# A cross-attention and expert kernel: the last sum of a group in two halves, reciprocals multiplied in one operation, and the work on x one slot later

## The chip, the core and the metric

The kernel runs on one core of a Trainium2 chip. The metric is device time of one execution, in microseconds. PE is the matrix engine, DVE, ACT and POOL are the vector, scalar and GpSimd engines, and SP issues most of the DMAs. A "block" is 128 rows.

## What is computed

Cut to what matters (four batches, 512 tokens of width 512, a context of 1601 rows):

```python
def attention(q, k, v):
    scores = jnp.einsum('bqhd,bkhd->bhqk', q, k) * scale
    probs = jax.nn.softmax(scores, axis=-1)
    return jnp.einsum('bhqk,bkhd->bqhd', probs, v)
q = rms_norm(linear(x, q_w, q_b), norm_q_w)            # 16 heads of 32
k, v = rms_norm(linear(ctx_txt, k_w, k_b), norm_k_w), linear(ctx_txt, v_w, v_b)
k_img, v_img = rms_norm(linear(ctx_img, ...)), linear(ctx_img, ...)
out = linear(attention(q, k_img, v_img) + attention(q, k, v), o_w, o_b)
x = x + out(_layernorm(x), ctx_2048)
x = x + moe(_layernorm(x))                             # 32 experts, top 4, and a shared expert
```

## The kernel before

The attention part works through the four batches (`one_pass`, p = 0; a second pass runs only for data with extreme scores). Each batch has a projection (`project` on each engine) and an attention stage (`attention` on PE, `exponentials` on ACT, `sums_and_results` on DVE). The expert part follows. Every engine has its own instruction stream, written out by hand, and semaphores join them; an engine never passes over an instruction that waits. The order of the work is therefore the order in which the calls stand in each engine's loop.

**Projection.** It has 17 slots, i = 0 to 16. Thirteen hold a block of the context (`KV_SLOT` = 0 to 7, 9, 11, 13, 15, 16), from which a key block and, one slot later, a value block are made; four (`Q_SLOT` = 8, 10, 12, 14) hold a block j = 0 to 3 of x, from which the queries are made. All operands of the products are split into a high and a low f16 part, so a product of 128 rows is 12 matmuls.

- The product of slot i is `key(i)` on PE. For a slot of x it waits for `x_out`, the landing of the turned block (`rows_turned` in `key`), and reads it from `xt`.
- Its result is taken out of PSUM by DVE in `key_raw(i)` (L796), squared and summed by ACT in `key_square(i)` (L628), scaled by POOL in `key_scale(i)` (L533, L536), normalized by DVE in `key_norm(i)` (L809, one slot later), cast by ACT in `key_high(i)` (L623), and its low part is made by DVE in `key_low(i)` (L815), which in DVE's stream stands in slot i+1 behind `key_raw(i+1)`. SP then turns it with a DMA transpose, `turn_key(i)` (L382), in slot i+1 too.
- The context block's own low part is `ctx_low` (L777) on DVE.
- A block of x goes through `x_stats` (L821, L822) on DVE, `x_scale` (L540, L541) on POOL, `x_normed` (L826) on DVE, `x_high` (L634) on ACT, `x_low` (L830) on DVE and `turn_x` (L387) on SP. In SP's slot the transpose of x stands behind `turn_key(i-1)`.
- In batches 1 to 3 the results of the batch before are finished in the same slots. `weigh` (L835, L836, L839) in slots 3 to 6 multiplies the numerators of a group, of image and text keys, by the reciprocals that a DMA has spread, and adds both; `out_low` (L844) follows. The output product, the residual's load (L364), the layer norm and the stores (L368, L372, L398) and a transpose (L393) stand in slots 8 to 16.

**Attention stage.** For each of four groups of four heads it passes over 13 key blocks (n = 0 to 12), so 52 steps s. PE makes the scores two steps ahead (`scores`, L1215), ACT the exponentials in two halves into one of four buffers (L718), PE the numerators (`weighted`, L1221). DVE adds the exponentials of the text keys up (`acc`, L972 and L975), so that PE can sum them over the rows with few matmuls (`text_part`, L1261). Image keys have their own sum (`image_sum`, L936) and their own copy of the numerators (L954). At n = 12 DVE waits for PE's last numerators, copies them out of PSUM (L963), which lets PE start the next group in that bank (`a_nt`), and adds the last exponentials (L975), which frees their buffer for ACT (`a_sum`). In batch 3 DVE also converts weights of the shared expert (`ffn_weight`, L869, L870) between groups.

Of the kernel before, what the change touches and what calls it, by code (L numbers as in the profile page):

```python
# [30 lines left out]
NG = HEADS // 4  # L31
# [132 lines left out]
def attention_program(nc, m, d, x1_dram, x2_dram, r_dram, table, out, s_turned, s_xr):  # L164

    with ExitStack() as ctx:
# [168 lines left out]
        def _(sp):  # L335
# [49 lines left out]
            def turn_x(bb, j):  # L385
                sp.wait_ge(x_lo, xn(bb, j))
                sp.dma_start_transpose(xt[:, j, :].rearrange("p (a k) -> p a k", k=P),  # L387
                                       xs[j % 2].rearrange("p s n -> p (s n)")).then_inc(x_out[j % 2], 16)
# [29 lines left out]
            def one_pass(p):  # L418
# [16 lines left out]
                for bb, b in passes(p):  # L435
                    if b > 0:
                        sp.wait_ge(c_lo, kvn(bb, 0))
                        load_ctx(bb, b, 2)
                    upto(sp, a_den, bb * NG)
                    q = out_batch(bb - 1) if b else None  # L440
                    for i in range(SLOTS):
                        if b > 0 and i == 1:
                            store_sums(bb - 1)
                        k = KV_AT.get(i)
                        if k is not None and k + 2 < KT and k > 0 and (b > 0 or k != 2):
                            sp.wait_ge(c_lo, kvn(bb, k))
                            load_ctx(bb, b, k + 2)
                        if b == 0 and k == 1:
                            sp.wait_ge(c_lo, kvn(bb, 2))
                            load_ctx(bb, b, 4)  # L450
                        if i == 4:
                            load_x(bb, b, 1)
                        if b == 0 and i == 1:
                            load_x(bb, b, 0)
                            load_weight(WQ)
                            if p == 0:
                                load_vec(QB, "qb", s_vq)
                                load_vec(QW, "qw", s_vq)
                        if bb == 0 and i == 4:
                            load_weight(WO)  # L460
                            sp.wait_ge(s_vq, 32)
                            load_vec(OB, "ob", s_vq)
                            sp.dma_start(vb2[:, 0, :], d["vb"]).then_inc(s_vq, 16)
                            sp.dma_start(vb2[:, 1, :], d["vib"]).then_inc(s_vq, 16)
                            sp.dma_start(mark[:, :, :], d["mark"]).then_inc(s_vq, 16)
                        if bb == 0 and i == 6:
                            sp.wait_ge(s_z0, 3)
                            zero = mxrow[:, :, :].rearrange("p g q -> p (g q)").bitcast(F32)
                            sp.dma_start(table[T:T + DUMMY, :], zero[:, 0:TROW]).then_inc(s_zero, 16)
                            sp.dma_start(out[T:T + DUMMY, :], zero[:, 0:D]).then_inc(s_zero, 16)  # L470
                        if i == 1 and b > 0:
                            load_x(bb, b, 0)
                        if i in (5, 6) and b > 0:
                            residual(q, b - 1, i - 5)
                        if i >= 1:
                            turn_key(bb, i - 1)
                        if b > 0 and i - 1 in LOW_SLOT:
                            store_turned(q, b - 1, LOW_SLOT.index(i - 1))
                        if b > 0 and i in NORM_SLOT:
                            j = NORM_SLOT.index(i)  # L480
                            store_norm(q, b - 1, j)
                            if j + 2 < QT:
                                residual(q, b - 1, j + 2)
                        if b > 0 and i in LOW_SLOT:
                            turn_out(q, LOW_SLOT.index(i))
                        if i in (5, 7, 9, 11):
                            turn_x(bb, (i - 5) // 2)
                        if b > 0 and i - 1 in O_SLOT:
                            store(q, b - 1, O_SLOT.index(i - 1))
                    if b + 1 < B:  # L490
                        first_loads(bb + 1, b + 1)
                    turn_key(bb, SLOTS - 1)
                    if b > 0:
                        store_turned(q, b - 1, QT - 1)
# [20 lines left out]
        def _(pool):  # L515
# [39 lines left out]
            def one_pass(p):  # L555
                for bb, b in passes(p):
                    for i in range(SLOTS):
                        if i in (3, 5, 7, 9):
                            x_scale(bb, (i - 3) // 2)
                        key_scale(bb, i)  # L560
                        if b > 0 and i in O_SLOT:
                            add_bias(out_batch(bb - 1), O_SLOT.index(i))
                        if b > 0 and i - 1 in O_SLOT:
                            out_scale(out_batch(bb - 1), O_SLOT.index(i - 1))
# [19 lines left out]
        def _(act):  # L584
# [67 lines left out]
            def project(p, bb, b):  # L652
# [8 lines left out]
                for i in range(SLOTS):  # L661
# [11 lines left out]
                    if b > 0 and WEIGH + 1 <= i < WEIGH + 1 + NG:  # L673
                        out_high(q, i - WEIGH - 1)
                        if i - WEIGH - 1 < 2:
                            spread(bb, i - WEIGH + 1)
                    if i in (4, 6, 8, 10):
                        x_high(bb, (i - 4) // 2)
                    if b == 0 and i <= 1:
                        ctx_high(bb, 2 + i)  # L680
                    key_square(bb, i)
# [63 lines left out]
        def _(dve):  # L745
# [86 lines left out]
            def weigh(q, g):  # L832

                dve.wait_ge(s_rb[g % 2], 64 * (2 * q + g // 2 + 1))
                image = own(dve.tensor_tensor(nums[:, g, 1, :], nums[:, g, 1, :], rb[:, g % 2, 1, :], ALU.mult))  # L835
                dve.tensor_tensor(nums[:, g, 0, :], nums[:, g, 0, :], rb[:, g % 2, 0, :], ALU.mult).then_inc(a_mt, 1)  # L836
                dve.wait_ge(d_link, image)
                dve.wait_ge(a_mt, gn(q, g))
                dve.scalar_tensor_tensor(nums[:, g, 0, :], nums[:, g, 1, :], vbias[:, g:g + 1], nums[:, g, 0, :],  # L839
                                         ALU.add, ALU.add).then_inc(a_at, 1)  # L840
# [32 lines left out]
            def project(p, bb, b):  # L873
                q = out_batch(bb - 1) if b else None
                for i in range(SLOTS):
# [7 lines left out]
                        out_norm(q, NORM_SLOT.index(i))  # L883
                    if b > 0 and i in LOW_SLOT[:QT - 1]:
                        norm_low(q, LOW_SLOT.index(i))
                    if i in (3, 5, 7, 9):
                        x_stats(bb, (i - 3) // 2)
                    if i in (4, 6, 8, 10):
                        x_normed(bb, (i - 4) // 2)
                    if i in (5, 7, 9, 11):  # L890
                        x_low(bb, (i - 5) // 2)
                    if bb == 0:
                        if i == 0:
                            dve.wait_ge(s_vi, 32)
# [46 lines left out]
            def sums_and_results(p, bb, b):  # L941
                fl = lambda t: t.rearrange("p h q -> p (h q)")
                for g in range(NG):
# [13 lines left out]
                    for n in range(4, KT):  # L957
                        s = s0 + n
                        dve.wait_ge(a_exp, unit(bb, 2 * s + 1))
                        cur = fl(prob[:, s % PROBS, :, :])  # L960
                        if n == KT - 1:
                            dve.wait_ge(a_av, step(bb, s))
                            dve.tensor_copy(nums[:, g, 0, :], ps[:, NUM, :]).then_inc(a_nt, 1)  # L963
                        if b == B - 1 and g == NG - 1 and n >= KT - PRODUCT_SUMS:
                            continue
                        if n == 4:
# [1147 lines left out]
```

## Time and profile before

| | us |
|---|---|
| Median of 3 runs | 1189.96 (1187.46 to 1190.88) |
| The profiled execution, its own time | 1194.59 |
| Its span, first to last instruction | 1192.8 |
| PE busy | 1116.2 (94%) |
| DVE busy | 856.9 (72%) |
| ACT busy | 650.6 (55%) |
| POOL busy | 202.1 (17%) |
| Mean granted clock of PE | 0.995 |

Busy times are shares of one execution whose stages have different limits, so they are to be read by stage. The projections end at about 92, 295, 498 and 701 us, the attention stages at about 201, 404, 607 and 814; the expert part takes the rest. PE's matmuls are pipelined, and a busy PE isn't PE at its peak. A wait names the instruction that came last by the profile.

### The profile page before, as it was taken

To read this page: it belongs to the slowest core of one execution; us is meant where nothing else is said; L and a number is where in the kernel's file an instruction comes from. 1 tells how busy PE (TensorE), PEld (TensorE's weight loads), DVE (VectorE), ACT (ScalarE), POOL (GpSimd) and SP (SyncE) were. 2 spreads that over 40 slices of the span, in tenths; PEclk is the share of its full clock that TensorE was granted. 3 is DMA by queue.
4 is the path that set the end of the run, shared out by engine and by line. 5 is a ranking of instruction groups with operands and counts; after the bars stand their busy time and mean duration, and the time that the engine had idled before them with its cause. 6 is when DMAs were issued, how large, how long until landed. Compare 5 with 4: busy or idle time off the path is not lost. (4 is left out here: it accounts for less than half of the span.)

```text
span 1192.8 us, 21823 instructions
## 1 busy us (share of the span) xinstructions
PE 1116.2 (94%) x8948; PEld 415.7 (35%) x8948; DVE 856.9 (72%) x1056; ACT 650.6 (55%) x916; POOL 202.1 (17%) x307
## 2 busy tenths in 40 slices
PE   7899999999999989999999999887999989999996
PEld 3342223344222334322233432222544433333332
DVE  6777889897898988788889879997789842222221
ACT  5559997444999644699955469883311121221121
POOL 1220000243000024300002430002100021333442
PEclk9999999999999999999999999999999999999999
DMA  8851000768200096900028780104813337999742
GB/s 299 199 109 43 2 2 10 194 135 201 54 2 2 20 228 136 203 8 2 2 72 194 171 215 31 36 3 136 359 60 109 113 113 285 348 317 313 215 62 33
DMA packets 142860, 150.15 MB, mean 126 GB/s; under 512 B 108833, under 2 KB 109089, under 8 KB 137761
## 3 DMA queue, kind: packets, MB, share of 16 engines
q1 hardware_dynamic: 135328, 131.57, 38.1%
q0 software_dynamic: 5120, 10.82, 4.9%
q10 hardware_dynamic: 2304, 6.29, 2.2%
q8 instruction: 72, 1.18, 0.4%
q14 instruction: 36, 0.29, 0.1%
HBM read 101.96 MB, written 21.51 MB: 104 GB/s over the span
## 5 line engine op out<-in xcount | busy, mean ns | idle before, releaser
L718 ACT ACTIVATE work<-ps 128x1024 f32<-128x1024 f32 x384 | 372.3, 1022 | 30.7 <-PE ps L1215 15.0
L1221 PE MATMUL ps<-work,vals 128*32 128x512 f32 (+2 forms) x1664 | 220.3, 600 | 3.8 <-DVE nums L963 2.1
L1072 PE MATMUL ps<-wts,work 128*128 128x512 f16 x864 | 194.9, 379 | 11.1 <-DVE work L777 10.7
L1215 PE MATMUL ps<-quer,keys 32*128 32x512 f16 x2496 | 171.9, 377 | 22.2 <-ACT work L718 14.9
L975 DVE TENSOR_TENSOR work<-work 128x2048 f32<-128x2048 f32 x64 | 146.6, 2291 | 6.2 <-ACT work L718 0.5
L975 DVE TENSOR_TENSOR attn<-attn,work 128x2048 f32<-128x2048 f32 x62 | 142.0, 2290 | 5.4 <-ACT work L718 0.5
L1072 PEld LDWEIGHTS ps<-wts,work 128*128 128x128 f16 x864 | 83.3, 98 | 118.7 <-issue 19.3
L2040 PE MATMUL ps<-wring,xgt 128*80 128x512 f32 x256 | 114.9, 592 | 0.0
L1866 DVE COPY xgt<-ps 128x320 f32<-128x320 f32 x32 | 15.7, 491 | 137.8 <-PE ps L2031 137.8
L1072 PE MATMUL ps<-wts,hl 128*128 128x512 f16 x432 | 101.1, 386 | 12.0 <-DVE wts L759 7.3
L533 POOL TENSOR_SCALAR small<-small 128x1 f32<-128x1 f32 x68 | 20.5, 301 | 534.9 <-ACT work L628 534.9
L1215 PEld LDWEIGHTS ps<-quer,keys 32*128 32x128 f16 x2496 | 46.3, 92 | 183.4 <-ACT work L718 149.9
L623 ACT CAST work<-work 128x512 f16<-128x512 f32 x68 | 42.0, 617 | 114.5 <-DVE work L809 114.4
L809 DVE SCALAR_TENSOR_TENSOR work<-work,small,vec 128x512 f32<-128x512 f32 (+1 forms) x72 | 59.4, 824 | 20.2 <-POOL small L536 20.2
L628 ACT ACTIVATE work<-work 128x512 f32<-128x512 f32 x68 | 42.8, 630 | 47.6 <-DVE work L796 47.6
L2055 PE MATMUL ps<-wring,ht 128*80 128x512 f32 x128 | 62.2, 608 | 6.4 <-ACT ht L1608 3.6
L1534 POOL DMA_INDIRECT out<-yf,idx x32 | 45.4, 1420 | 131.7 <-DMA out<-yf,idx 102.3
L1072 PEld LDWEIGHTS ps<-wts,hl 128*128 128x128 f16 x432 | 41.8, 99 | 68.2 <-issue 20.9
L2040 PEld LDWEIGHTS ps<-wring,xgt 128*80 128x80 f32 x256 | 38.4, 150 | 71.1 <-issue 70.9
L1613 ACT ACTIVATE yf<-ps,xg 80x512 f32<-80x512 f32 x32 | 21.9, 683 | 71.0 <-PE ps L2055 47.7
L1221 PEld LDWEIGHTS ps<-work,vals 128*32 128x32 f32 (+2 forms) x1664 | 38.7, 108 | 58.8 <-issue 52.7
L1608 ACT COPY ht<-ps 128x160 f32<-128x160 f32 x32 | 9.3, 291 | 77.8 <-PE ps L2048 77.8
(221 smaller groups left out, 1402.5 us busy)
## 6 DMA issues: line engine op xcount, KB each, us to landing
wring<-in_wx SPq DMA_DIRECT2D x32, 1536.0 KB, 9.1
raw<-in_ctx SPq DMA_DIRECT2D x52, 256.0 KB, 3.3
rb<-sums_inverse ACTq DMA_DIRECT2D x48, 128.0 KB, 3.8
work<-in_x SPq DMA_DIRECT2D x8, 512.0 KB, 4.8
table<-nums SPq DMA_DIRECT2D x16, 256.0 KB, 2.5
work<-in_x SPq DMA_DIRECT2D x12, 256.0 KB, 3.5
x<-work SPq DMA_DIRECT2D x12, 256.0 KB, 2.6
x2t_rows<-nums SPq DMA_DIRECT2D x12, 256.0 KB, 2.5
```

Source lines behind the costliest of these rows:

```text
L623: act.copy(stack[i % 2][:, 0, :], kraw[i % 2]).then_inc(k_hi, 1)
L628: act.activation(junk, kraw[i % 2], ACT.Square, accum_out=ssq[i % 2]).then_inc(k_sq, 1)
L718: act.activation(prob[0:rows, s % PROBS, 2 * half:2 * half + 2, :], ps[0:rows, 2 * pair:2 * pair + 2, :], ACT.Exp, scale=SCALE, bias=pad i ...
L809: ins = dve.scalar_tensor_tensor(kraw[i % 2][a:z, :], kraw[i % 2][a:z, :], rin[i % 2][a:z, :], vec[a:z, weight, :], ALU.mult, ALU.mult)
L975: dve.tensor_tensor(acc, acc, cur, ALU.add).then_inc(a_sum, 1)
L1072: mm = pe.matmul(out, lhs(a, c)[:, cols], wts[:, w, z, c * D:(c + 1) * D], start=(k == 0), stop=(k == len(steps) - 1))
L1215: mm = pe.matmul(ps[:, 2 * pair + h % 2, :], k[h * HD:(h + 1) * HD, :], q[h * HD:(h + 1) * HD, :], start=(e == 0), stop=(e == len(terms) - 1))
L1221: return pe.matmul(ps[h * HD:(h + 1) * HD, NUM, :], vals[a:z, ORDER[n], g * P + h * HD:g * P + (h + 1) * HD], prob[a:z, s % PROBS, h, :], ...
L1534: pool.indirect_dma_start(out=out[:, :], out_offset=bass.IndirectOffsetOnAxis(ap=idx[:, n:n + 1], axis=0), in_=yf[n % RESULTS][:, :], in_o ...
L1613: act.activation(yf[n % RESULTS][:, :], ps[0:CAP, 2 + n % 2, :], ACT.Copy, scale=xg[n % GATHERS][:, D + n:D + n + 1]).then_inc(m_yf, 1)
L2040: mm = pe.matmul(ps[0:CAP, 7 if n % 2 == 0 else 0, :], xgt[n % 2][:, c, :], wring[n % RING][:, c * D:(c + 1) * D], start=(c == 0), stop=(c ...
L2055: mm = pe.matmul(ps[0:CAP, 2 + n % 2, :], ht[n % 2][:, c, :], wring[n % RING][:, (NC + c) * D:(NC + c + 1) * D], start=(c == 0), stop=(c = ...
```

## The change

1. At n = 12 the addition of 2048 columns becomes two of 1024, one ahead of the wait for PE's numerators and their copy, one behind. Only the second signals `a_sum`. The last group of batch 3, which has no such addition, stays as it was.
2. In `weigh` one multiplication of 128x1024 takes the place of two of 128x512.
3. The steps of a block of x move one slot on, on DVE, POOL, ACT and SP. PE's slots of x stay.

```diff
--- before.py
+++ after.py
@@ -483,8 +483,8 @@
                                 residual(q, b - 1, j + 2)
                         if b > 0 and i in LOW_SLOT:
                             turn_out(q, LOW_SLOT.index(i))
-                        if i in (5, 7, 9, 11):
-                            turn_x(bb, (i - 5) // 2)
+                        if i in (6, 8, 10, 12):
+                            turn_x(bb, (i - 6) // 2)
                         if b > 0 and i - 1 in O_SLOT:
                             store(q, b - 1, O_SLOT.index(i - 1))
                     if b + 1 < B:
@@ -555,8 +555,8 @@
             def one_pass(p):
                 for bb, b in passes(p):
                     for i in range(SLOTS):
-                        if i in (3, 5, 7, 9):
-                            x_scale(bb, (i - 3) // 2)
+                        if i in (4, 6, 8, 10):
+                            x_scale(bb, (i - 4) // 2)
                         key_scale(bb, i)
                         if b > 0 and i in O_SLOT:
                             add_bias(out_batch(bb - 1), O_SLOT.index(i))
@@ -674,8 +674,8 @@
                         out_high(q, i - WEIGH - 1)
                         if i - WEIGH - 1 < 2:
                             spread(bb, i - WEIGH + 1)
-                    if i in (4, 6, 8, 10):
-                        x_high(bb, (i - 4) // 2)
+                    if i in (5, 7, 9, 11):
+                        x_high(bb, (i - 5) // 2)
                     if b == 0 and i <= 1:
                         ctx_high(bb, 2 + i)
                     key_square(bb, i)
@@ -832,9 +832,8 @@
             def weigh(q, g):
 
                 dve.wait_ge(s_rb[g % 2], 64 * (2 * q + g // 2 + 1))
-                image = own(dve.tensor_tensor(nums[:, g, 1, :], nums[:, g, 1, :], rb[:, g % 2, 1, :], ALU.mult))
-                dve.tensor_tensor(nums[:, g, 0, :], nums[:, g, 0, :], rb[:, g % 2, 0, :], ALU.mult).then_inc(a_mt, 1)
-                dve.wait_ge(d_link, image)
+                both = nums[:, g, :, :].rearrange("p t q -> p (t q)")
+                dve.tensor_tensor(both, both, rb[:, g % 2, :, :].rearrange("p t q -> p (t q)"), ALU.mult).then_inc(a_mt, 1)
                 dve.wait_ge(a_mt, gn(q, g))
                 dve.scalar_tensor_tensor(nums[:, g, 0, :], nums[:, g, 1, :], vbias[:, g:g + 1], nums[:, g, 0, :],
                                          ALU.add, ALU.add).then_inc(a_at, 1)
@@ -883,12 +882,12 @@
                         out_norm(q, NORM_SLOT.index(i))
                     if b > 0 and i in LOW_SLOT[:QT - 1]:
                         norm_low(q, LOW_SLOT.index(i))
-                    if i in (3, 5, 7, 9):
-                        x_stats(bb, (i - 3) // 2)
                     if i in (4, 6, 8, 10):
-                        x_normed(bb, (i - 4) // 2)
+                        x_stats(bb, (i - 4) // 2)
                     if i in (5, 7, 9, 11):
-                        x_low(bb, (i - 5) // 2)
+                        x_normed(bb, (i - 5) // 2)
+                    if i in (6, 8, 10, 12):
+                        x_low(bb, (i - 6) // 2)
                     if bb == 0:
                         if i == 0:
                             dve.wait_ge(s_vi, 32)
@@ -959,8 +958,15 @@
                         dve.wait_ge(a_exp, unit(bb, 2 * s + 1))
                         cur = fl(prob[:, s % PROBS, :, :])
                         if n == KT - 1:
+                            parted = not (b == B - 1 and g == NG - 1)
+                            if parted:
+                                dve.wait_ge(a_sum, added(bb, g, n - 5))
+                                dve.tensor_tensor(acc[:, 0:2 * L], acc[:, 0:2 * L], cur[:, 0:2 * L], ALU.add)
                             dve.wait_ge(a_av, step(bb, s))
                             dve.tensor_copy(nums[:, g, 0, :], ps[:, NUM, :]).then_inc(a_nt, 1)
+                            if parted:
+                                dve.tensor_tensor(acc[:, 2 * L:], acc[:, 2 * L:], cur[:, 2 * L:], ALU.add).then_inc(a_sum, 1)
+                                continue
                         if b == B - 1 and g == NG - 1 and n >= KT - PRODUCT_SUMS:
                             continue
                         if n == 4:
```

On SP, slots 9 and 10 of the projection of batch 1. L387 turns a block of x, L382 a key or query block, L372 stores to the table, L364 loads the residual. Before:

```order
L382 DMA_TRANSPOSE quer<-work 128x8x128 [waits k_lo]
L387 DMA_TRANSPOSE work<-work 128x8x128 [waits x_lo]
L368 DMA x<-work 128x512 [waits o_out]
L382 DMA_TRANSPOSE keys<-work 128x8x128 [waits k_lo]
L372 DMA table<-nums 128x512 [waits n_norm]
L364 DMA work<-in_x 128x512 [waits s_st0,n_norm]
L368 DMA x<-work 128x512 [waits o_out]
```

And now:

```order
L382 DMA_TRANSPOSE quer<-work 128x8x128 [waits k_lo]
L368 DMA x<-work 128x512 [waits o_out]
L382 DMA_TRANSPOSE keys<-work 128x8x128 [waits k_lo]
L372 DMA table<-nums 128x512 [waits n_norm]
L364 DMA work<-in_x 128x512 [waits s_st0,n_norm]
L387 DMA_TRANSPOSE work<-work 128x8x128 [waits x_lo]
L368 DMA x<-work 128x512 [waits o_out]
```

The transpose of x's block 2 went from behind the query block of slot 8 to behind the key block of slot 9 and two further DMAs.

On DVE, slots 9 and 10 of the same projection (L848, L853, L854, L859 of the change are L849, L854, L855, L860 of before). Before:

```order
L821 BN_STATS small<-work 128x6
L822 BN_AGGR small<-small 128x2
L830 TENSOR_TENSOR work<-work 128x512
L796 SCALAR_TENSOR_TENSOR work<-ps,vec 128x512
L815 TENSOR_TENSOR work<-work 128x512
L849 SCALAR_TENSOR_TENSOR work<-ps,work 128x512
L854 BN_STATS small<-work 128x6
L855 BN_AGGR small<-small 128x2
L777 TENSOR_TENSOR hl_62<-raw,hl_62 128x512
L809 SCALAR_TENSOR_TENSOR work<-work,small,vec 128x512
L860 TENSOR_SCALAR nums<-work,small 128x512
L826 TENSOR_SCALAR work<-work,small 128x512
```

And now:

```order
L796 SCALAR_TENSOR_TENSOR work<-ps,vec 128x512
L815 TENSOR_TENSOR work<-work 128x512
L848 SCALAR_TENSOR_TENSOR work<-ps,work 128x512
L853 BN_STATS small<-work 128x6
L854 BN_AGGR small<-small 128x2
L777 TENSOR_TENSOR hl_62<-raw,hl_62 128x512
L809 SCALAR_TENSOR_TENSOR work<-work,small,vec 128x512
L859 TENSOR_SCALAR nums<-work,small 128x512
L821 BN_STATS small<-work 128x6
L822 BN_AGGR small<-small 128x2
L830 TENSOR_TENSOR work<-work 128x512
L796 SCALAR_TENSOR_TENSOR work<-ps,vec 128x512
```

The next row of the first piece is the L796 of slot 10. The statistics and the subtraction for x stood ahead of the L796 of slot 9 and now stand ahead of that of slot 10, where the normalizing (L826) was.

On DVE, the first group end of batch 0. Before:

```order
L972 TENSOR_TENSOR work<-work 128x2048
L975 TENSOR_TENSOR work<-work 128x2048 x7
L963 COPY nums<-ps 128x512
L975 TENSOR_TENSOR work<-work 128x2048
L936 TENSOR_TENSOR image<-work 128x2048
```

And now:

```order
L978 TENSOR_TENSOR work<-work 128x2048
L981 TENSOR_TENSOR work<-work 128x2048 x7
L964 TENSOR_TENSOR work<-work 128x1024
L966 COPY nums<-ps 128x512
L968 TENSOR_TENSOR work<-work 128x1024
L935 TENSOR_TENSOR image<-work 128x2048
```

The copy of the numerators now has a half addition on each side.

## Rows read from the trace of the kernel before

**Rows 1.** Windows: a projection, an attention stage; columns as in the first row.
```profile
core 0: us, PE busy (x) PEld busy (x) DVE busy (x) ACT busy (x) POOL busy (x), PEclk, DMA share, GB/s
200.70:295.50 94.80, 90.16 (x461) 39.30 (x458) 80.55 (x121) 40.65 (x88) 29.94 (x54) 1.00 0.69 163
310.00:400.00 90.00, 86.12 (x1192) 23.98 (x1192) 81.10 (x42) 84.81 (x88) 0.00 (x0) 1.00 0.02 5
```

**Rows 2.** PE's timeline, projection of batch 1: start, us, instructions, [idle before <-releaser].
```profile
241.89 2.75 PE L1072 MATMUL ps<-wts,work 128*128 128x512 f16 x12 [1.18 <-DVE work L777]
...
247.06 5.34 PE L1072 MATMUL ps<-wts,work 128*128 128x512 f16 x24
...
260.01 5.34 PE L1072 MATMUL ps<-wts,work 128*128 128x512 f16 x24
...
267.78 2.75 PE L1072 MATMUL ps<-wts,work 128*128 128x512 f16 x12
```

**Rows 3.** SP's timeline (its DMA issues), the same projection.
```profile
244.09 2.29 SPq L382 DMA_TRANSPOSE keys<-work  x1
...
265.85 1.26 SPq L382 DMA_TRANSPOSE keys<-work  x1
...
267.83 0.38 SPq L364 DMA_DIRECT2D work<-in_x  x1
```

**Rows 4.** The transposes of x (L387): last line of that line's own view.
```profile
DMA to landing us min/median/max: 3.1/3.2/5.1
```

**Rows 5.** DVE's timeline, the same projection, slots 6, 9 and 10.
```profile
243.38 0.68 DVE L815 TENSOR_TENSOR work<-work 128x512 f16<-128x512 f32 x1
...
257.00 0.68 DVE L821 BATCH_NORM_STATS2 small<-work 128x6 f32<-128x512 f32 x1
...
258.39 0.68 DVE L796 SCALAR_TENSOR_TENSOR work<-ps,vec 128x512 f32<-128x512 f32 x1
...
264.08 0.54 DVE L826 TENSOR_SCALAR work<-work,small 128x512 f32<-128x512 f32 x1
264.54 0.69 DVE L796 SCALAR_TENSOR_TENSOR work<-ps,vec 128x512 f32<-128x512 f32 x1
265.14 0.68 DVE L815 TENSOR_TENSOR work<-work 128x512 f16<-128x512 f32 x1
```

**Rows 6.** PE's timeline, projection of batch 0.
```profile
59.56 7.93 PE L1072 MATMUL ps<-wts,work 128*128 128x512 f16 x36 [0.70 <-DVE work L777]
...
70.86 2.75 PE L1072 MATMUL ps<-wts,work 128*128 128x512 f16 x12 [0.39 <-DMA work<-work]
```

**Rows 7.** SP's timeline, projection of batch 0.
```profile
50.53 1.71 SPq L382 DMA_TRANSPOSE keys<-work  x1
```

**Rows 8.** DVE's timeline, projection of batch 0.
```profile
61.04 0.68 DVE L815 TENSOR_TENSOR work<-work 128x512 f16<-128x512 f32 x1
```

**Rows 9.** DVE's timeline, first group end of batch 0.
```profile
122.97 0.69 DVE L963 COPY nums<-ps 128x512 f32<-128x512 f32 x1 [0.76 <-PE ps L1221]
123.58 2.28 DVE L975 TENSOR_TENSOR work<-work 128x2048 f32<-128x2048 f32 x1
```

**Rows 10.** ACT's timeline behind the same group end.
```profile
125.98 1.94 ACT L718 ACTIVATE work<-ps 128x1024 f32<-128x1024 f32 x2 [0.32 <-DVE work L975]
...
132.91 1.94 ACT L718 ACTIVATE work<-ps 128x1024 f32<-128x1024 f32 x2 [0.83 <-PE ps L1215]
```

**Rows 11.** PE's timeline, end of group 1 in batch 3.
```profile
761.48 1.07 PE L1221 MATMUL ps<-work,vals 128*32 128x512 f32 x8 [1.03 <-DVE nums L963]
```

**Rows 12.** PE's timeline behind its two longest waits after the start.
```profile
829.07 2.04 PE L1900 MATMUL ps<-rcp,sel 128*128 128x512 f32 x2 [5.48 <-PEq L166]
...
984.59 0.47 PE L2031 MATMUL ps<-identf,xg 80*128 80x80 f32 x4 [2.70 <-DVE xgt L1866]
```

**Rows 13.** Windows over the same two places; the next to last columns hold clock.
```profile
828.00:832.00 4.00, 2.93 (x4) 1.41 (x5) 2.04 (x4) 0.62 (x1) 1.28 (x8) 0.61 0.18 29
984.00:988.00 4.00, 3.42 (x14) 1.56 (x15) 0.93 (x3) 0.00 (x0) 0.00 (x0) 0.74 0.74 215
```

## The prediction

> **What bounds the kernel now.** I read the stretches first, because the two kinds of stage have different limits. Between two attention stages lies a projection of 94.8 us in which PE is busy for 90.16 us; in attention ACT is busy for 84.81 of 90.00 us, PE for 86.12 and DVE for 81.10 [rows 1]. So a projection is a PE stage: a change counts there if it makes PE wait longer or shorter. Attention is an ACT stage with PE and DVE close behind.
>
> Next, PE's timeline in the projection of batch 1 [rows 2]. Slots are numbered i = 0 to 16. The row at 241.89 is key(7), and its 1.18 us of waiting ends with a DVE subtraction (L777): in slots 3 to 6 DVE is the slower engine. The row at 247.06 is key(8), the first product that reads a turned block of x; 260.01 is key(10) and 267.78 is key(12), which read blocks 1 and 2. None of these waits. Call their starts T8, T10 and T12.
>
> Then SP's queue [rows 3] with the landing times [rows 4]: a turned block of x lands 3.2 us after its issue. The row at 265.85 is the turning of key(9) in slot 10, which waits for key_low(9) on DVE, the row at 265.14 [rows 5]. It is followed by two more DMAs of slot 10, the last at 267.83 for 0.38 us.
>
> **The move of x by a slot.** Per block it moves five steps: two DVE statistics and the POOL scale behind them, the DVE normalizing, ACT's cast, DVE's subtraction, and the transpose on SP. Nothing is added or removed, but PE's use of the blocks stays in slots 8, 10, 12 and 14. The transpose must now follow the turning of a key in its own, later slot: turn_x(2) used to follow turn_key(8), which waits for key_low(8), and now follows turn_key(9). And key_low(9) stands on DVE behind key_raw(10), which needs PE's key(10) to be finished. So the new loop is: key(10) on PE, key_raw(10) and key_low(9) on DVE, turn_key(9) and turn_x(2) on SP, landing, key(12).
>
> Its smallest length in batch 0, where nothing else is queued: 2.75 (product) + 0.05 + 0.60 + 0.68 (raw, low) + 0.03 + 1.28 (one transpose's issue and the step to the next) + 3.2 (landing) + 0.15 (PE's start after its releaser) = 8.74 us. PE itself needs three products of 2.59 from one x product to the next, 7.77 us. The loop therefore exceeds PE's work. In batches 1 to 3 two further DMAs lie in it, about 1.0 us, so at least 9.7 us.
>
> Batches 1 to 3, with the clock of batch 1:
> - T8. From slot 3 to key_low(5) in slot 6 DVE has one normalizing less, 0.46, and three merged multiplications, 0.06 each (below). key_low(5) moves from 243.38 to about 242.8 [rows 5]. turn_key(5) is issued at 243.5 and takes 1.24 at best (here 2.29 [rows 3]); turn_x(0) follows at 244.8, lands at 248.0, and PE starts at 248.15 instead of 247.06: +1.1, or +2.1 with the long transpose. DVE's relief up to key(7), one pair of statistics and subtraction less (1.39, see T12) and 0.1 of the multiplications, so 1.5 us at most, is swallowed whole, since PE now waits behind it for block 0.
> - T10 is natural, 261.1: block 1 lands at about 258.5.
> - T12. In slots 8 to 10, ahead of key_raw(10), DVE carried one pair of statistics and subtraction, 1.39 (257.00 to 258.39), and two normalizings of 0.46 (264.08 to 264.54) [rows 5]; now two pairs and one normalizing, 0.93 more. Key_raw(9) waits 0.33 for the later key(9). So key_low(9) ends at 267.1 instead of 265.82, turn_key(9) follows, turn_x(2) is issued 2.4 later at 269.5 behind the table's store and the residual's load, lands at 272.7, and PE starts at 272.9 instead of 267.78: +5.1. As some of DVE's short waits will close up, I take **4.8 per batch, 14.4 for three**. The bounds are +1.9 (no backlog on DVE, T10 unmoved: 9.7 against 7.77) and +6.1.
> - T14 needs block 3 at about 285.5 and has it by 285.4: nothing more, though without reserve.
>
> Batch 0 [rows 6 to 8]. Here block 2 already ends a wait of 0.39 before T12 (70.86). Block 0 now follows turn_key(5), issued at 50.53 and then, with a pair in place of a normalizing ahead of it, at about 51.1: it lands at 55.6, T8 is 55.75 (today about 53.5). Block 1 now follows key_low(7), 61.04 plus 1 of extra x work plus 0.68, so 62.8; plus 1.3 to its issue and 3.2 to its landing: T10 is 67.4 instead of 62.15 (59.56 and one product). Two loops of 8.74 follow: T14 is 84.9 instead of 78.6 (three products after 70.86). **+6.3**; bounds +3.3 (T8 at 55.75 and three smallest loops, 82.0) and +7.
>
> **The addition in two halves.** At a group's end DVE waits 0.76 for PE, copies the numerators, then adds 2.29 us [rows 9]. A half addition (128x1024) should take 1.22: 0.68 for 512 columns [rows 5] and 2.28 for 2048 give 0.53 per 512 more. It fills the 0.76 and overshoots: the copy moves from 122.97 to 123.44, +0.47, the addition's end from 125.86 to 125.27, -0.59. ACT's wait of 0.32 for the addition [rows 10] seems to go. But PE starts the next group's numerators 0.15 after the copy, so the scores of the next tile but one end at about 126.1 instead of 125.6, and ACT gets them at 126.16 instead of 125.98. The next two tiles are then within 0.05 of today, and the 0.83 that ACT waits for scores at 132.91 follows PE, which is 0.03 later. Ten group ends: **0**, bounds -0.3 and +0.2 each. At the end of a batch the last sum is not what PE waits for: 0. In batch 3, where the FFN weights' conversion leaves DVE behind, PE already waits 1.03 for the copy [rows 11]; there the copy comes 1.23 later, and the next group, which runs at DVE's pace, loses 0.95. Two such places: **+1.9**, bounds 0 and 2.5.
>
> **Reciprocals in one operation.** 12 multiplications fewer; from the first one to the sum behind them took 1.39 and will take 1.22 + 0.11: 0.06 each. It lies in slots 3 to 6, already counted, and is swallowed with the relief: 0.
>
> **The clock.** A stall of four microseconds may have a price of its own. After 5.48 us without matmuls the granted clock of 828 to 832 is 0.61, most of it at the lower of the two levels (1.2 GHz instead of 2.4); after a wait of 2.70 it is 0.74 in the stretch that holds the end of the wait [rows 12, 13]. The first is (1 - 0.61) x 4 = 1.6 us of PE's work lost. The new stalls are about 3.9 us long, one in each batch (268.9, when PE has done its work, to 272.8; 63.5 to 67.4 in batch 0).  A stall of 3.9 after dense work lies between, so I take two of four: **+3.2**, bounds 0 and 6.4.
> The Trainium skill ("TensorE: Matmul & The Clock Gate", Part 1) says that the throttled state is the default and that activity releases it. By that rule every one of the four stalls loses the clock, and the sum would be 3.2 higher; both rows of this trace agree with it.
>
> **Sum.** 6.3 + 14.4 + 1.9 + 3.2 = 25.8, less about 0.8 for the last wait of a projection, where DVE will have caught up a little: +25. Against the profiled execution's own time of 1194.59 that is 1219.6; the median of the runs, 1189.96, lies 4.6 lower, and the same step gives **1215**.
>
> **Rivals.**
> 1. Mild: DVE has no backlog left when key(10) ends, because the stall itself gives it time. The loops then have their smallest lengths, 3.3 + 3 x 1.9 = 9: 1199. For it: DVE idles 15% of the projection [rows 1]. Against: the order on DVE puts the moved pair directly ahead of key_raw(10), so time gained earlier doesn't help. Chance 0.12.
> 2. Faster: DVE's relief reaches PE, 1.5 us in three projections, and twelve waits of 0.32 for the addition go: -8.3, 1181.7. It decides at one point: turn_x(2) must be issued before 264.4 to land before 267.78 (and turn_x(0) before 243.7). Against it, key(10) itself ends at 262.76 and 2.6 us of DVE and SP work lie between. Chance 0.04, with all that could be faster.
> 3. The gains and the late blocks cancel within 0.3%, about what a measurement of this kernel can tell from no change. It needs the late blocks to cost 3 us or so in all, less than batch 0's smallest loops alone. Chance 0.04.
> 4. The clock is lost at each stall, and the long transposes come too: 1221. This is the upper part of my own case.
>
> The forecast has 0.80. The range, 1203 to 1224, takes in all of it and half of the mild rival. Faster 0.04, same 0.04, slower 0.92.
>
> **What would show it.** PE's wait ahead of key(12) is released by the DMA that writes a block of x, 3 to 5 us in each batch, and in batch 0 ahead of key(10) too. The wait ahead of key(7) is below 0.3. In attention the copy follows a half addition without a wait, ACT's 0.32 is about the same or moved, and the two last group ends of batch 3 are longer. I am wrong if no wait of PE on such a DMA passes 1 us, or if projections are shorter than 94 us.

## The result, and the profile after

The change takes **1228.92 us** (median of 6 runs, 1226.3 to 1232.46) and the kernel before 1191.18 in the same session (6 runs, 1187.46 to 1192.05): a ratio of **1.0323 [1.0299, 1.0348]**. The direction is the forecast's; the time lies 13.9 us above the 1215 and 4.9 above the upper end of the range, 1224. The profiled execution has an own time of 1230.48 and a span of 1228.7.

The page of the changed kernel, busy time of the engines, the granted clock in 40 slices, and the group of the projection's products:

```profile
PE 1130.3 (92%) x8948; PEld 418.7 (34%) x8948; DVE 858.7 (70%) x1059; ACT 652.2 (53%) x916; POOL 205.2 (17%) x307
...
PEclk9999999988999999899999999999899999999999
...
L1078 PE MATMUL ps<-wts,work 128*128 128x512 f16 x864 | 207.8, 397 | 32.8 <-DMA work<-work 25.3
```

The wait that had a total of 0.4 us (once, in batch 0 [rows 6]) is now the largest of the projection: eight times, 25.3 us together, for the DMA that turns a block of x. A ninth, ahead of key(8) in batch 0, is named `issue` in the rows; but SP issued turn_x(0) at 52.97, 3.31 us before that wait ends, so it is of the same kind:

```profile
56.28 9.62 PE L1078 MATMUL ps<-wts,work 128*128 128x512 f16 x36 [2.04 <-issue]
67.94 5.34 PE L1078 MATMUL ps<-wts,work 128*128 128x512 f16 x24 [2.04 <-DMA work<-work]
```

The matmuls of the group also have more busy time, 397 ns each where it was 379. Windows of the changed kernel, the projection of batch 1 and the stretches behind its two stalls (columns as in [rows 1]):

```profile
208.03:314.19 106.16, 95.44 (x461) 40.31 (x458) 80.70 (x118) 40.97 (x86) 31.05 (x54) 0.94 0.64 146
254.00:258.00 4.00, 2.19 (x6) 0.82 (x7) 3.40 (x7) 3.19 (x7) 0.74 (x2) 0.62 0.89 175
258.00:262.00 4.00, 4.00 (x12) 1.36 (x11) 2.31 (x6) 0.76 (x2) 1.08 (x2) 0.53 0.01 2
282.00:286.00 4.00, 1.12 (x3) 0.44 (x4) 2.78 (x6) 2.36 (x6) 0.74 (x2) 0.53 1.13 261
286.00:290.00 4.00, 4.00 (x13) 1.49 (x12) 1.43 (x3) 0.61 (x1) 0.00 (x0) 0.62 1.11 206
```

The projection took 94.80 us before [rows 1] and takes 106.16: 6.1 us more in which PE does nothing, and 5.3 more in which the same 461 matmuls take longer, since the clock is granted at 0.94. PE's timeline of the changed kernel, the same projection:

```profile
250.16 2.75 PE L1078 MATMUL ps<-wts,hl 128*128 128x512 f16 x12
255.81 8.27 PE L1078 MATMUL ps<-wts,work 128*128 128x512 f16 x24 [2.90 <-DMA work<-work]
...
271.69 5.34 PE L1078 MATMUL ps<-wts,work 128*128 128x512 f16 x24
276.87 2.75 PE L1078 MATMUL ps<-wts,hl 128*128 128x512 f16 x12
284.88 4.81 PE L1078 MATMUL ps<-wts,work 128*128 128x512 f16 x12 [5.26 <-DMA work<-work]
```

The row at 255.81 is key(8), 271.69 is key(10) and 284.88 key(12). There are **two** stalls in the batch, not one, and matmuls behind each run at the lower level: 24 take 8.27 us (5.34 in [rows 2]), 12 take 4.81 (2.75). What SP and DVE do ahead of them in the changed kernel, SP first:

```profile
250.71 1.24 SPq L382 DMA_TRANSPOSE keys<-work  x1
252.39 1.24 SPq L387 DMA_TRANSPOSE work<-work  x1
...
277.71 1.24 SPq L382 DMA_TRANSPOSE keys<-work  x1
278.99 0.57 SPq L372 DMA_DIRECT2D table<-nums  x1
279.66 0.38 SPq L364 DMA_DIRECT2D work<-in_x  x1
280.09 1.24 SPq L387 DMA_TRANSPOSE work<-work  x1
```

```profile
250.00 0.68 DVE L815 TENSOR_TENSOR work<-work 128x512 f16<-128x512 f32 x1
...
274.54 0.55 DVE L859 TENSOR_SCALAR nums<-work,small 128x512 f32<-128x512 f32 x1 [0.44 <-POOL small L547]
275.00 0.69 DVE L821 BATCH_NORM_STATS2 small<-work 128x6 f32<-128x512 f32 x1
...
276.39 0.69 DVE L796 SCALAR_TENSOR_TENSOR work<-ps,vec 128x512 f32<-128x512 f32 x1
277.00 0.68 DVE L815 TENSOR_TENSOR work<-work 128x512 f16<-128x512 f32 x1
```

The loop of the forecast is there step by step. Key(10) ends at 274.3; the moved pair (275.00) keeps key_raw(10) until 276.39; key_low(9) ends at 277.68; turn_key(9), the table's store and the load of the residual put turn_x(2) at 280.09, 2.38 behind turn_key(9) (2.4 was said); PE starts 4.79 later. That last step was said to be 3.35.

### The profile page after: what moved, and what is told of

Its sections match the earlier page's. It is cut to its first block and busy times, and to the rows that moved or that the text cites. A ratio compares the mean times of both kernels' runs of the same rounds, so it can differ in the third digit from the quotient of the medians.

```text
span 1228.7 us, 21814 instructions
## 1 busy us (share of the span) xinstructions
PE 1130.3 (92%) x8948; PEld 418.7 (34%) x8948; DVE 858.7 (70%) x1059; ACT 652.2 (53%) x916; POOL 205.2 (17%) x307
## 3 DMA queue, kind: packets, MB, share of 16 engines
q8 instruction: 72, 1.18, 0.4%
## 5 line engine op out<-in xcount | busy, mean ns | idle before, releaser
L1078 PE MATMUL ps<-wts,work 128*128 128x512 f16 x864 | 207.8, 397 | 32.8 <-DMA work<-work 25.3
L981 DVE TENSOR_TENSOR work<-work 128x2048 f32<-128x2048 f32 x56 | 128.4, 2292 | 6.3 <-DVE work L981 0.5
L981 DVE TENSOR_TENSOR attn<-attn,work 128x2048 f32<-128x2048 f32 x55 | 126.0, 2292 | 5.4 <-ACT work L718 0.4
L533 POOL TENSOR_SCALAR small<-small 128x1 f32<-128x1 f32 x68 | 23.0, 338 | 575.5 <-ACT work L628 575.5
L796 DVE SCALAR_TENSOR_TENSOR work<-ps,vec 128x512 f32<-128x512 f32 (+1 forms) x72 | 49.4, 686 | 34.4 <-PE ps L1078 34.1
L2046 PEld LDWEIGHTS ps<-wring,xgt 128*80 128x80 f32 x256 | 38.4, 150 | 71.1 <-issue 70.9
```

The source lines that it names most:

```text
L796: ins = dve.scalar_tensor_tensor(kraw[i % 2][a:z, :], bank[a:z, :], 1.0 / WS, vec[a:z, bias, :], ALU.mult, ALU.add)
L981: dve.tensor_tensor(acc, acc, cur, ALU.add).then_inc(a_sum, 1)
L1078: mm = pe.matmul(out, lhs(a, c)[:, cols], wts[:, w, z, c * D:(c + 1) * D], start=(k == 0), stop=(k == len(steps) - 1))
L2046: mm = pe.matmul(ps[0:CAP, 7 if n % 2 == 0 else 0, :], xgt[n % 2][:, c, :], wring[n % RING][:, c * D:(c + 1) * D], start=(c == 0), stop=(c ...
```

## The experiments

All ratios are to the kernel before, run on the same chip. The table has the stages of the profiled executions, in us. A projection is taken from the last exponential of one batch to the first of the next. "Lower" is the time at the 1.2 GHz level up to the end of the projection of batch 3, attention left out.

| kernel | start to attention 0 | projections 1, 2, 3 | attention 3 | lower |
|---|---|---|---|---|
| before | 92.6 | 94.80, 94.32, 94.14 | 113.22 | 0 |
| the change | 99.6 | 106.16, 103.11, 102.74 | 115.55 | 34.1 |
| x's move alone | 99.2 | 103.85, 103.41, 102.77 | 113.20 | 23.9 |
| halves alone | 94.4 | 93.15, 93.49, 93.01 | 118.35 | 0 |
| multiplication alone | 93.4 | 92.70, 92.54, 93.03 | 113.22 | 0 |
| transposes alone | 102.6 | 102.57, 100.56, 99.32 | 113.23 | 20.5 |
| filled, no halves in batch 3 | 100.7 | 99.89, 99.77, 99.67 | 113.23 | 0 |
| SP's order turned | 96.8 | 93.66, 93.47, 92.99 | 119.21 | 3.4 |

The projections of the kernel before are rather long in this one execution: with the halves alone, which changes nothing in them, they take 93.0 to 93.5 us. So a difference of 1 us or so from its row need not be an effect of a change.

**First question: which part costs the time.** The change with x back in its old slots on all four engines (here SP's part), and the kernel before with x's move alone:

```diff
-                        if i in (6, 8, 10, 12):
-                            turn_x(bb, (i - 6) // 2)
+                        if i in (5, 7, 9, 11):
+                            turn_x(bb, (i - 5) // 2)
```

> The change with the work on x put back into its old slots; the half additions and the merged multiplication stay. Late blocks of x (my theory): nearly the whole loss goes. What is left is batch 3, where the copy behind a half addition cost 2.3 us in the profile of the change, so 1193 to 1194. Rival (the half additions shift every engine's phase and cost time in all groups): above 1205. Second rival (only the clock matters and it falls anyway): no lower level in the projections of this run, so this one is refuted if the granted clock is 1.0 up to the end of batch 3.

Measured: 1195.4, ratio 1.0042 [1.0021, 1.0062]. Nearly the whole loss goes; the rest is 1.4 us more than was said, since the wait in batch 3 cost clock as well (below).

> The kernel before with nothing but the work on x one slot on. Late blocks: the loss of the change less the 2.3 us of batch 3, so about 1226, with PE's waits for the DMA of x ahead of key(8) and key(12) as in the change, and the clock at its lower level behind them. Rival (it takes the three parts together): below 1212.

Measured: 1224.12, ratio 1.0283 [1.0251, 1.0314]. So x's move is nearly all of it. All six stalls of batches 1 to 3 in this kernel (2.40 to 4.92 us) are followed by the lower level, each for 3.4 us. Batch 3, key(8):

```profile
678.42 7.00 PE L1072 MATMUL ps<-wts,work 128*128 128x512 f16 x24 [2.40 <-DMA work<-work]
```

The other two parts one at a time (each is the kernel before with that hunk of the diff):

> The kernel before with the last addition of a group in halves and nothing else. By the profile of e1: nothing in batches 0 to 2 (0.1 us each at most), and in batch 3, where DVE is behind, PE waits over 2 us longer at two group ends for the copy. If that wait keeps the clock up: +2.3 us, 1192.5; if it lowers it once, as in e1: +5.3, 1195.5. Rival (the half additions take ACT's waits away, as meant): below 1188.

Measured: 1196.96, ratio 1.005 [1.0036, 1.0063]: the half additions alone make the kernel slower. This is 1.5 us above the worse of the two expected values.

> The kernel before with the one multiplication of 128x1024 and nothing else. 0.06 us for each of three groups ahead of key(7) in three projections, if anything: within 0.6 us of before. Rival (the merged form also saves the wait between the two multiplications and the sum, so that PE's waits in slots 4 to 7 close): 1187 to 1189.

Measured: 1188.2, ratio 0.9982 [0.9965, 0.9999]: the interval just leaves out no change, and the median lies in the rival's range. From the first multiplication to the start of the sum takes 1.26 us (242.83 to 244.09 in this kernel's trace) instead of 1.39, so 0.13 less, where 0.06 was said; PE's wait ahead of key(7) is 1.04 instead of 1.18. This is the only version that was run whose interval lies below no change.

**Where the halves cost.** In batches 0 to 2 an attention stage is 0.28, 0.08 and 0.08 us longer, in batch 3 2.3 or over 5. At the first group end of the change ACT waits 0.50 us, for PE's scores, where it waited 0.32 for the addition [rows 10]: the wait has moved, not gone. Batch 3 of the kernel with x back, DVE and then PE at the end of group 1, and the window behind it:

```profile
759.70 1.22 DVE L964 TENSOR_TENSOR attn<-attn,work 128x1024 f32<-128x1024 f32 x1
760.85 0.68 DVE L966 COPY nums<-ps 128x512 f32<-128x512 f32 x1
```

```profile
761.67 1.30 PE L1227 MATMUL ps<-work,vals 128*32 128x512 f32 x8 [2.36 <-ACT work L718]
762.91 1.47 PE L1221 MATMUL ps<-quer,keys 32*128 32x512 f16 x12
```

```profile
764.00:768.00 4.00, 4.00 (x32) 0.71 (x36) 0.86 (x1) 2.24 (x3) 0.00 (x0) 0.50 0.00 0
```

PE's wait for the copy is 2.36 us where it was 1.03 [rows 11]; the row names ACT, but the wait ends 0.15 behind the copy. In this run and in the one with the halves alone (118.50 and 118.35 us for the stage) the clock then fell for 6.8 us. There are two waits of 2.36 us in the stage, and in four of the five profiles that have them the clock fell behind one of the two; in the profiled run of the change it fell behind neither, and the stage took 115.55.

**Second question: is the stall's length the whole price, or the clock behind it.** The change, with useless matmuls (fillers) into an unused bank of PSUM while PE would wait ahead of key(8) and key(12); they change no output:

```diff
                     j = Q_AT[i]
+                    for k in range((8, 0, 16, 0)[j]):
+                        pe.matmul(ps[:, 4, :], ident[:, :], wts[:, WKI, 0, 0:D], start=True, stop=True)
```

> The change, with matmuls whose result nobody reads put ahead of PE's wait for a block of x: 8 of 512 columns ahead of key(8), 16 ahead of key(12), into an unused bank (1.7 and 3.5 us, less than the waits there). The blocks land as late as before. If the lower clock behind the stalls costs time of its own (theory: PE bounds the projection, so it does), it stays at 1.0 in the projections and the time falls by 12 to 17 us, to 1212 to 1217. If the loop over DVE and SP sets the time anyway (rival), the clock stays up and the time falls by less than 4 us, 1225 or more. If the extra matmuls delay the products behind them, it is above 1229.

Measured: 1221.1, ratio 1.0254 [1.0223, 1.0285]. PE's timeline and windows of this kernel, the projection of batch 1:

```profile
256.03 1.89 PE L1105 MATMUL ps<-wts,ident 128*128 128x512 f16 x8
259.11 5.35 PE L1078 MATMUL ps<-wts,work 128*128 128x512 f16 x24 [1.19 <-DMA work<-work]
...
279.84 3.62 PE L1105 MATMUL ps<-wts,ident 128*128 128x512 f16 x16
284.99 2.76 PE L1078 MATMUL ps<-wts,work 128*128 128x512 f16 x12 [1.53 <-DMA work<-work]
```

```profile
258.00:262.00 4.00, 2.89 (x14) 1.36 (x15) 3.36 (x6) 3.07 (x7) 0.74 (x2) 1.00 0.68 149
286.00:290.00 4.00, 4.00 (x21) 1.78 (x19) 2.82 (x5) 1.34 (x3) 0.59 (x2) 1.00 0.95 232
```

The block arrives as late as ever, but the 24 matmuls take 5.35 again and the clock stays at 1.00. The projections are 5.5, 3.5 and 3.4 us shorter than the change's: more work on PE, less time. Batch 0 gets 3.6 longer: the sixteen fillers ahead of key(12) take 3.62 us where the change waited 0.80, and behind a wait of 2.65 ahead of key(10), which has none, the clock still falls. With that, and with the clock lost in batch 3's attention (118.44 us), the whole gained 7.8 us and not the 12 to 17 expected: a miss in size, though 1221.1 is also below the rival's 1225. To see the late blocks alone, this kernel got eight fillers ahead of key(10) in batch 0 too, and no half additions in batch 3:

```diff
-                            parted = not (b == B - 1 and g == NG - 1)
+                            parted = b < B - 1
```

> e5 with two further repairs: 8 matmuls of filling ahead of key(10) in batch 0, where e5 still lost the clock for 3.4 us, and no half addition in batch 3, where the wait of 2.4 us for the copy was followed by 6.8 us at the lower level. If the parts add (theory): 1221.1 less 1.7 and less 5.2, so 1214 to 1215, with no lower clock before 814 us; what is left over 1190 is the late blocks alone. If something else in the change costs time (rival), it stays above 1218.

Measured: 1215.8, ratio 1.0223 [1.0201, 1.0246], 0.8 above what was said. No stretch of the four projections is at the lower level, and batch 3's attention takes 113.23 as before. What is left, about 26 us, is the waiting itself (in batch 0 with some filling that is longer than the wait was).

**Third question: why the blocks are late, DVE's order or SP's.** The change, with turn_x put ahead of turn_key in SP's slot and nothing else:

```diff
+                        if i in (6, 8, 10, 12):
+                            turn_x(bb, (i - 6) // 2)
                         if i >= 1:
                             turn_key(bb, i - 1)
...
-                        if i in (6, 8, 10, 12):
-                            turn_x(bb, (i - 6) // 2)
```

> The change, with SP's transpose of a block of x ahead of the transpose of the key in the same slot. The block then waits only for its own subtraction on DVE, which stands ahead of the key's raw copy. If the queue order on SP is what makes the blocks late (theory): block 2 of batch 1 is issued some 3.5 us earlier, PE's wait ahead of key(12) falls from 5.3 to below 2 us, the one ahead of key(8) goes, the clock stays up, and the time is 1195 to 1202. If the order on DVE alone makes it late (rival): waits of over 3 us stay and the time is above 1212.

Measured: 1197.6, ratio 1.0069 [1.0045, 1.0094]. Of the 38 us, 30 are gone. SP's and PE's timelines in this kernel, batch 1, slot 10 and key(12):

```profile
267.52 1.24 SPq L387 DMA_TRANSPOSE work<-work  x1
268.80 1.33 SPq L382 DMA_TRANSPOSE keys<-work  x1
270.18 0.58 SPq L372 DMA_DIRECT2D table<-nums  x1
```

```profile
262.21 5.34 PE L1078 MATMUL ps<-wts,work 128*128 128x512 f16 x24
...
270.91 2.75 PE L1078 MATMUL ps<-wts,work 128*128 128x512 f16 x12 [0.77 <-DMA work<-work]
```

The transpose of x no longer waits for key_low(9) and the two DMAs; key(12) waits 0.77 us and its 12 matmuls take 2.75. In batch 0 a stall ahead of key(10) stays, with 3.4 us at the lower level behind it:

```profile
65.56 7.03 PE L1078 MATMUL ps<-wts,work 128*128 128x512 f16 x24 [2.57 <-DMA work<-work]
```

There turn_x(1) is issued at 62.18, right behind the subtraction of x that ends at 62.15, so in batch 0 it is DVE's order that makes this block late. The opposite test leaves DVE, ACT and POOL as they were before and moves SP's transposes alone:

> The kernel before with nothing moved but SP's transpose of a block of x: it stands one slot later, all work on DVE, ACT and POOL where it was. If the place in SP's queue makes the blocks late (theory, after e6): nearly the loss of e2, 1218 to 1225, with waits for the DMA of x ahead of key(8) and key(12). If the pair of DVE operations ahead of the key's raw copy is what makes them late (rival): below 1205.

Measured: 1217.96, ratio 1.0239 [1.0213, 1.0264]. PE's timeline of this kernel, batch 1:

```profile
259.04 5.34 PE L1072 MATMUL ps<-wts,work 128*128 128x512 f16 x24 [2.09 <-DMA work<-work]
...
283.23 5.28 PE L1072 MATMUL ps<-wts,work 128*128 128x512 f16 x12 [3.32 <-DMA work<-work]
```

Both stalls are there with DVE's order untouched. So in batches 1 to 3 the place behind turn_key in SP's queue is the cause, and DVE's later order adds to it (2.90 and 5.26 against 2.09 and 3.32).

**Is there a version that gains.** First, SP's order turned, and batch 3's copy ahead of a whole addition:

> e6 (SP turns the block of x before the key) without the half addition in batch 3. If the 7.5 us that e6 was behind are that wait with its clock, and batch 0: about 5.9 go and it is 1191 to 1193. If they are in the projections (rival): 1196 or more.

Measured: 1191.99, ratio 1.0022 [1.0004, 1.004], as said: the price of the halves in batch 3 comes off on top of that of SP's order. What is left is batch 0, where key(10) still waits 2.56 us. Then the idea at its best: the merged multiplication, no halves, batch 0 in its old slots, x one slot on in batches 1 to 3, with SP's order turned there:

```diff
+X_STATS = [[3, 5, 7, 9], [4, 6, 8, 10]]
...
-                        if i in (3, 5, 7, 9):
-                            x_scale(bb, (i - 3) // 2)
+                        if i in X_STATS[b > 0]:
+                            x_scale(bb, X_STATS[b > 0].index(i))
```

> Merged multiplication, no half additions; the work on x one slot on in batches 1 to 3 alone, with SP's transpose of a block of x ahead of the key's. In e6 PE then had key(8) 2.2 us earlier than before in each of these batches and lost 0.9 at key(12). Late blocks (theory): 1.3 us gained in three batches, 1186 to 1187. Rival (DVE's relief is given back later in the projection, since slots 9 to 16 are bound by DVE and ACT too): 1190 or more.

Measured: 1190.55, ratio 1.0 [0.9986, 1.0014]. A miss: no gain, and not even that of the multiplication. Key(12) starts 8.62 to 8.68 us behind key(10) in batches 1 to 3, instead of 7.77. And the 2.2 us at key(8) on which the expectation rested were counted against the long projections of the kernel before: here key(8) starts 37.5 us behind key(1) on the average, with the multiplication alone 36.9. The last one moved only blocks 0 and 1, so that block 2 is in time:

```diff
-X_STATS = [[3, 5, 7, 9], [4, 6, 8, 10]]
+X_STATS = [[3, 5, 7, 9], [4, 6, 7, 9]]
```

> As e7, but in batches 1 to 3 only blocks 0 and 1 of x are worked on one slot later (statistics in slots 4, 6, 7, 9), and the steps of two blocks in one slot stand in the order subtraction, normalizing, statistics. Block 2 lands when it did before, so the 0.9 us at key(12) should go: 1183 to 1185. Rival (two normalizings and statistics meet in slots 7 and 8, and DVE's backlog there delays key(9) or key(10)): no better than e7.

Measured: 1191.71, ratio 1.0022 [1.0002, 1.0042]. Again a miss. Key(12) is in time (7.77), but key(16) now starts 9.02 us behind key(14), where it was 7.77, and waits for a subtraction on DVE:

```profile
288.07 2.75 PE L1078 MATMUL ps<-wts,hl 128*128 128x512 f16 x12 [1.09 <-DVE hl L781]
```

Key(8) is only 0.2 us earlier here, on the average, than with the multiplication alone; what the moved work gives in slots 3 to 6 is smaller than the wait that it makes later in the same projection.

## Why the prediction missed

The two profiled executions differ by 35.9 us (1230.48 and 1194.59), where the sum said 25. By its terms:

- **Late blocks, batches 1 to 3: 14.4 said, 16.1 found** (the filled kernel's projections, 299.33 us, less 283.26 before). T8: +1.1 said; against the same profiled execution key(8) starts, counted from key(1), 1.42, 0.48 and 2.14 us later in the change. T12: from key(8) to key(12) 3.7 more was said (4.8 less 1.1), and the filled kernel has 5.2, 4.6 and 4.3 more. The mis-sized number is the landing: the median of 3.2 us [rows 4] was taken for a transpose that is issued among other DMAs. From turn_x(2) to key(12) it took 4.79 us in batch 1 (280.09 to 284.88), 4.40 in batch 2 and 3.85 in batch 3, where 3.35 was said. The upper bound, the 5.1 of the same row, was in my hands. T14 was right: behind key(12) it keeps its distance of 12.95 in the filled kernel.
- **Batch 0: 6.3 said, 7.0 found.** Right in size, in part by luck: 1.7 of the 7.0 are clock (the 36 matmuls behind key(8)'s wait take 9.62 us, not 7.93), which the forecast had in another term. One stall of 3.9 ahead of key(10) was said; the waits are 2.04 (key(8)), 2.04 (key(10)) and 1.07 us (key(14)).
- **The clock: 3.2 said, 12.7 found** (the change's projections 1 to 3, 312.01 us, less the filled kernel's 299.33). This is the step that failed, and twice: in how many stalls there are, and in what each costs. I wrote "the new stalls are about 3.9 us long, one in each batch". But my own T8 term said that 1.5 us of relief at key(7) is swallowed and key(8) is 1.1 later still: that is a stall of 2.6 us, and I priced it as waiting only. So there were eight stalls of 2 us and more, not four. And the price of 1.6 came from a row where the lower level lasted 3.4 us; here it lasted 6.8 in four cases of five. Of the six stalls of batches 1 to 3 five were followed by it, 2.1 us lost per stall on the average. Counted directly, by what the steps from key(8) to key(10) and from key(12) to key(14) take beyond 12.95 us, it is 11.2 us; the other 1.5 are blocks that came somewhat later than in the filled kernel. The "two of four" was too mild for long stalls: in the thirteen profiles every wait of PE of 2.56 us or more (after the first 30 us of the span) was followed by the lower level. The Trainium skill ("TensorE: Matmul & The Clock Gate", Part 1) has the throttled state as the default, released by activity. The forecast set aside the reading of it by which every stall loses the clock; the runs are nearer to that reading (five of six here, six of six with x's move alone) than to my two of four, though the wait of 2.44 us in batch 3 kept the clock at 1.00.
- **The halves: 1.9 said, 2.8 found.** Ten group ends at 0 were right (0.44 us in all, in batches 0 to 2). The half additions take 1.22 us each, as worked out. In batch 3 PE's wait ahead of the next group is 2.36 instead of 1.03 us, twice, and the stage 2.33 longer, where 1.9 was said; that this wait, too, can cost the clock (2.8 to 3.7 us more in four other profiles) I had not seen.
- **The rest of the span: 0.8 off said, 2.7 off found.** The 0.8 stood for the last wait of a projection; what was found lies where the change touches nothing: the part behind the last attention stage took 378.8 us in the profiled execution before, the longest of the thirteen profiles (the others 373.5 to 377.3), and 376.1 in that of the change.
- **From the profiled execution to the median: 4.6 off said, 1.6 found.** The change's profiled run lies 1.6 above its median. That the same step holds for both kernels was the second wrong assumption. The excess of the profiled run before lies in the last part, as just said, and in the projections: key(8) starts 38.4 us behind key(1) (three batches), and 37.2 on the average of nine batches in the three kernels that keep the old slots and were run later. The difference arises between key(3) and key(5), 12.0 to 12.7 us against 10.9 to 11.3 with the halves alone; ahead of key(7) both wait 1.18. Why that execution was longer there, no run shows.

The terms add up: 9.5 (clock) + 1.7 + 0.7 + 0.9 - 1.9 + 3.0 = 13.9 us above the forecast. The rivals: the mild one fails where the forecast said it would, since the moved pair stands directly ahead of key_raw(10) in the rows at 275.00 and 276.39, and DVE had idled before them. DVE's relief is small: in the two kernels with SP's order turned throughout, key(7) comes 1.1 us earlier than in the old-slot runs, on the average of six batches against nine, and key(12) gives 0.9 of it back. In the two later kernels key(7) is 0.1 later and 0.6 earlier than in the old-slot runs, so that even the 1.1 is not certain.

## What to carry to other kernels

When a step moves by a slot, list for each in-order queue what it now stands behind, and ask what that neighbour waits for: here DVE's order alone would have cost 0.8 to 0.9 us a batch in batches 1 to 3 (and more in batch 0), and the place behind one transpose on SP cost the rest. Where a sum says that one engine's relief is swallowed by a later wait, that is a new stall of both together; price its clock as well as its length, and ask of each stall on PE whether dense work stands around it. A saving that empties an engine in one part of a stage is worth nothing until the next wait in that stage is looked up.

## What the runs showed of the hardware

- In the thirteen profiles, TensorE's clock fell behind every wait of 2.56 us or more, the first 30 us of the span left out. Of the nineteen between 1.97 and 2.44 us it fell behind nine: of two waits of 2.04 in batch 0 of the change behind the first, behind 2.40 and not behind 2.44, and behind waits of 2.36 in some profiles and not in others. The same edit's price so varies by some 3 us between runs at one place alone.
- Lower stretches here last 3.4 us or 6.8, once 10.2. Useless matmuls in the gap avoided them in all six stalls of batches 1 to 3, in two kernels, even where up to 1.6 us of the wait remained.
- A transpose of a block of x between two places in SBUF holds SP for 1.24 to 1.33 us at the median and lands 3.2 us after its issue at the median. Behind the key's transpose, a store and a load, block 2's in batches 1 to 3 of the change came in 3.7 to 4.7 us after its issue; put ahead of the key's transpose, in 3.2 to 3.3. The Trainium skill ("DMA: Bandwidth & Descriptors", "Anatomy of one DMA") gives a fixed part of about 2.0 us for a DMA issued from GpSimd; no row here separates that part.
